# Two sparse expert layers: expert rows weighed at once and scattered with adding transfers onto stored residual rows

## What is computed

```python
x = x + gat(layernorm(x))
x = x + ffn0(layernorm(x))
x = x + gnn(layernorm(x))
x = x + ffn1(layernorm(x))

def ffn0(x):
    xn = norm(x) * gamma + beta
    top_vals, top_idx = top_k(xn @ Wr + br, 2)
    w = softmax(top_vals)                  # two shares for each node
    y = 0
    for e in range(8):
        h = gelu(xn @ W1[e] + b1[e])
        y = y + (h @ W2[e] + b2[e]) * w_full[..., e]
    return y
```

## Time and profile before

| | us |
|---|---|
| median of 3 runs | 3489.4 (3482.19 to 3492.77) |
| profiled execution, time | 3492.24 |
| profiled execution, span | 3490.5, mean granted TensorE clock 0.857 |

### The profile page before, as it was taken

One profiled execution on the slowest core, in us unless ns is written; L12 is line 12 of the kernel. 1 busy time (PEld: TensorE's weight loads), 2 busy tenths in 40 slices (PEclk: granted clock), 3 DMA queues, 4 the chain that ended last, 5 costly groups with the idle time before them and its releaser, 6 DMA issues. The chain is left out here.

```text
span 3490.5 us, 51176 instructions
## 1 busy us (share of the span) xinstructions
PE 2505.2 (72%) x12468; PEld 2001.2 (57%) x12469; DVE 1590.9 (46%) x3485; ACT 1320.4 (38%) x2875; POOL 1903.3 (55%) x2005
## 2 busy tenths in 40 slices
PE   5466666666666446999708888878888878649993
PEld 4344444444444435888607777767776744437772
DVE  5366666666666750111184444444444454621115
ACT  4544444444443223444343332332332324624441
POOL 0477777777775273222207777777777710553331
PEclk9688888887887557999959999999999999769996
DMA  5455555555553353222355555555555510432226
GB/s 154 126 140 140 143 140 140 144 140 141 144 140 94 100 194 100 82 82 84 112 184 167 159 158 153 158 159 153 158 159 152 151 32 2 140 130 85 91 85 251
DMA packets 319924, 459.47 MB, mean 132 GB/s; under 512 B 56729, under 2 KB 213962, under 8 KB 319498
## 3 DMA queue, kind: packets, MB, share of 16 engines
q0 software_dynamic: 94560, 261.75, 25.3%
q1 hardware_dynamic: 212888, 180.18, 17.6%
q10 hardware_dynamic: 12276, 15.62, 1.3%
HBM read 376.96 MB, written 80.39 MB: 131 GB/s over the span
## 5 line engine op out<-in xcount | busy, mean ns | idle before, releaser
L604 POOL DMA_INDIRECT room<-h_table,src_idx x784 | 749.1, 955 | 355.9 <-issue 238.3
L2182 POOL DMA_INDIRECT em_msg<-xn_table,src_idx x784 | 747.4, 953 | 337.5 <-issue 337.5
L1109 PE MATMUL at_ps<-room,at_member 128*128 128x264 f32 x1568 | 491.9, 468 | 68.7 <-DVE room L965 63.5
L2258 PE MATMUL em_pse<-em_We,em_attr_t 128*128 128x256 f32 x1552 | 396.1, 413 | 157.7 <-DVE em_msg L2206 157.7
L2206 DVE TENSOR_TENSOR em_msg<-em_pse,em_msg 128x1024 f32<-128x1024 f32 x196 | 230.8, 1219 | 551.3 <-DMA em_msg<-xn_table,src_idx 551.3
L2311 ACT ACTIVATE em_msg<-em_msg 128x1024 f32<-128x1024 f32 x196 | 207.2, 1057 | 682.7 <-DVE em_msg L2206 675.5
L2258 PEld LDWEIGHTS em_pse<-em_We,em_attr_t 128*128 128x128 f32 x1552 | 311.5, 206 | 226.4 <-DVE em_msg L2206 171.8
L1109 PEld LDWEIGHTS at_ps<-room,at_member 128*128 128x128 f32 x1568 | 339.6, 228 | 150.0 <-DVE room L965 82.1
L2265 PE MATMUL em_psa<-em_msg,em_member 128*128 128x256 f32 x1584 | 359.7, 380 | 4.4 <-DVE acc L2216 4.4
L2265 PEld LDWEIGHTS em_psa<-em_msg,em_member 128*128 128x128 f32 x1584 | 302.0, 191 | 46.2 <-DVE acc L2216 4.8
L1814 POOL DMA_INDIRECT y_table<-room,m0e_dest x104 | 99.7, 959 | 297.9 <-DVE room L1834 291.5
(11 more groups left out here) (402 smaller groups left out, 3863.0 us busy)
## 6 DMA issues: line engine op xcount, KB each, us to landing
em_attr<-in_edge_attr_dram SPq DMA_DIRECT2D x97, 512.0 KB, 4.2
room<-x_sorted SPq DMA_DIRECT2D x105, 258.0 KB, 2.7
at_dst_row<-dst_flat SPq DMA_DIRECT2D x98, 256.0 KB, 4.0
room<-h_table,src_idx POOLq DMA_INDIRECT x784
at_resets<-reset_flat SPq DMA_DIRECT2D x784, 8.0 KB
em_msg<-xn_table,src_idx POOLq DMA_INDIRECT x784, 2.8
room<-in_x_dram SPq DMA_DIRECT2D x12, 896.0 KB, 10.2
cn_rows<-y_table SPq DMA_DIRECT2D x5, 1792.0 KB, 10.2
```

The costliest lines, as they stand in the source:

```text
L604: pool.indirect_dma_start(msg[:, s, j, :], None, mem.h_table[:, :], bass.IndirectOffsetOnAxis(ap=mem.src_idx[:, c:c + 1].bitcast(u32), axi ...
L1109: ins = nc.tensor.matmul(sums[which], member[which][:, j, :], msg[:, s, c, :], start=(j == 0), stop=(j == CB - 1))
L2182: pool.indirect_dma_start(msg[:, s, j, :], None, mem.xn_table[:, :], bass.IndirectOffsetOnAxis(ap=mem.src_idx[:, c:c + 1].bitcast(u32), ax ...
L2258: ins = nc.tensor.matmul(ps_e[h][:, j, :], attr_t[:, s % 2, c * P:(c + 1) * P], We[:, :], start=True, stop=True)
```

## The change

The expert rows are multiplied by their share where they leave the experts, and the scatter adds them in HBM onto the residual row.

- Routing: as soon as a block's statistics are made, SP stores its residual rows to `m.target`, which is `y_table` for m0 (now one row for each node) and the output for m1. The shares are computed block by block: DVE makes `diff` in `choose`, ACT's new step `share(n)` the exponential as the last step of block n, and DVE the first share in `place`, into a third extra float of each scattered row. ACT's `share(n)` waits for `choose(n)`.
- Experts: DVE gets the destination by a copy, the share by two small operations (the second expert's share is one minus the first), and after the bias one multiplication for each tile. A new semaphore `y_taken` is set after the bias and is what PE waits for; `y_ready` is set after the multiplication. The scatter adds, and in m1 rows past the last node are dropped by a check of bounds.
- Home: m0 only loads the summed rows into `mem.X`, all loads issued at once, and goes on with the statistics. m1 has no such stage.

```diff
-XW = D + 2
+XW = D + 3
@@ phase_route, sync
+            for n in range(NR):
+                sp.wait_ge(var_ready, n + 1)
+                end = min((n + 1) * RT, m.target_rows // P)
+                sp.dma_start(m.target[n * RT * P:end * P, :].rearrange("(t p) f -> p t f", p=P),
+                             mem.X[:, n * RT:end, :]).then_inc(started, 16)
...
@@ phase_route, vector: choose and place
+                v.tensor_tensor(diff[:, tiles], top[1][:, tiles], top[0][:, tiles], ALU.subtract).then_inc(exp_in, 1)
...
+                dve.wait_ge(exp_done, n + 1)
+                chain(v.tensor_scalar(sums[:, tiles], ex[:, tiles], 1.0, None, ALU.add))
+                chain(v.reciprocal(xs[:, n % BUFS, :, D + 2], sums[:, tiles]))
                 dve.sem_inc(pos_ready, 1)
...
-            v.tensor_tensor(diff[:, :], top[1][:, :], top[0][:, :], ALU.subtract).then_inc(exp_in, 1)
-            dve.wait_ge(exp_done, 1)
-            chain(v.tensor_scalar(sums[:, :], ex[:, :], 1.0, None, ALU.add))
-            chain(v.reciprocal(m.w12[:, :, 0], sums[:, :]))
-            chain(v.tensor_tensor(m.w12[:, :, 1], m.w12[:, :, 0], ex[:, :], ALU.mult))
@@ phase_route, scalar
+            def share(n):
+                act.wait_ge(exp_in, n + 1)
+                tiles = slice(n * RT, (n + 1) * RT)
+                nc.scalar.activation(ex[:, tiles], diff[:, tiles], ACT.Exp).then_inc(exp_done, 1)
...
                     take_y(n + 3)
                 elif n == 0:
                     take_biases()
+                share(n)
@@ phase_experts, gpsimd
-                    pool.indirect_dma_start(mem.y_table[:, :], bass.IndirectOffsetOnAxis(ap=dest[:, j:j + 1].bitcast(u32), axis=0),
-                                            y[:, j, :], None).then_inc(sent, 16)
+                    pool.indirect_dma_start(m.target[:, :], bass.IndirectOffsetOnAxis(ap=dest[:, j:j + 1].bitcast(u32), axis=0),
+                                            y[:, j, :], None, bounds_check=m.last_row, oob_is_err=m.last_row is None,
+                                            compute_op=ALU.add).then_inc(sent, 16)
@@ phase_experts, vector
-                nc.vector.scalar_tensor_tensor(dest[:, :], of[:, :, 1], float(e), of[:, :, 0],
-                                               op0=ALU.not_equal, op1=ALU.add).then_inc(dest_ready, 1)
+                nc.vector.tensor_copy(dest[:, :], of[:, :, 0])
+                nc.vector.scalar_tensor_tensor(signed[:, :], of[:, :, 1], float(e), of[:, :, 2],
+                                               op0=ALU.not_equal, op1=ALU.subtract).then_inc(signed_ready, 1)
+                dve.wait_ge(signed_ready, g + 1)
+                nc.vector.scalar_tensor_tensor(share[:, :], signed[:, :], -1.0, signed[:, :],
+                                               op0=ALU.mult, op1=ALU.max).then_inc(dest_ready, 1)
                 for j in range(ET):
                     dve.wait_ge(y_done, g * ET + (j + 1))
-                    nc.vector.tensor_tensor(y[:, j, :], ps_y[:, j % 2, 0:D], m.b_last[:, e, :], ALU.add).then_inc(y_ready, 1)
+                    nc.vector.tensor_tensor(y[:, j, :], ps_y[:, j % 2, 0:D], m.b_last[:, e, :], ALU.add).then_inc(y_taken, 1)
+                    if j == 0:
+                        dve.wait_ge(dest_ready, g + 2)
+                    dve.wait_ge(y_taken, g * ET + (j + 3))
+                    nc.vector.tensor_scalar(y[:, j, :], y[:, j, :], share[:, j:j + 1], None, ALU.mult).then_inc(y_ready, 1)
@@ phase_experts, tensor
-                    pe.wait_ge(y_ready, g * ET + (j + 1))
+                    pe.wait_ge(y_taken, g * ET + (j + 1))
@@ phase_combine: removed
@@ phase_combine_norm: combine and weigh removed, loads straight into X
-            for n in range(1, BUFS):
+            for n in range(1, STEPS):
                 load(n)
             for n in range(STEPS):
-                if n + BUFS < STEPS:
-                    load(n + BUFS)
                 store(n)
```

More of the change, by code:

```diff
@@ L1346, in _ @@
                     load_x(n)
+            for n in range(NR):
[3 more added lines that the diff above has]
+                             mem.X[:, n * RT:end, :]).then_inc(started, 16)
+                if (n + 1) * RT * P > m.target_rows:
+                    sp.dma_start(m.target[end * P:m.target_rows, :], mem.X[0:m.target_rows - end * P, end, :]).then_inc(started, 16)
+            if m.attention is not None:
                 sp.wait_ge(heads_read, NR)
@@ L1822, in _ @@
             dve.sem_inc(y_ready, 2)
+            dve.sem_inc(y_taken, 2)
             dve.sem_inc(y_free, 1)
@@ L1897, in _ @@
             groups(act, group)
-def phase_combine(nc, mem, m, out=None):
-    TC, BUFS = 7, 3
-    SIZES = (3, 7, 7, 7, 7, 7, 5, 4, 2)
-    BLOCKS = [(sum(SIZES[:n]), nt) for n, nt in enumerate(SIZES)]
-    STEPS = len(BLOCKS)
-    with ExitStack() as ctx:
-        sb = lambda n, s, d=fp32: ctx.enter_context(nc.sbuf_tensor(f"{m.name}c_{n}", s, d))
-        sem = lambda n: new_semaphore(nc, mem, ctx, f"{m.name}c_{n}")
-        rows = sb("rows", [P, BUFS, TC, 2, D])
-        added, taken, stored = sem("added"), sem("taken"), sem("stored")
-        rows_in = [sem(f"rows_in{s}") for s in range(BUFS)]
-        block = ctx.enter_context(nc.Block(no_gpsimd_drain=True))
-        @block.vector
-        def _(dve):
-            for n, (t0, nt) in enumerate(BLOCKS):
-                s = n % BUFS
-                dve.wait_ge(rows_in[s], 16 * (n // BUFS + 1))
-                for w in range(2):
-                    for j in range(nt):
-                        t = t0 + j
-                        ins = nc.vector.scalar_tensor_tensor(tile_at(mem.X, t), rows[:, s, j, w, :], m.w12[:, t, w:w + 1],
-                                                             tile_at(mem.X, t), op0=ALU.mult, op1=ALU.add)
-                    if w == 0:
-                        ins.then_inc(added, 1)
-                        dve.wait_ge(added, n + 1)
-                ins.then_inc(taken, 1)
-            dve.wait_ge(taken, STEPS)
-        def load(eng, n):
-            t0, nt = BLOCKS[n]
-            s = n % BUFS
-            if n >= BUFS:
-                eng.wait_ge(taken, n - BUFS + 1)
-            at = t0 * P * 2
-            eng.dma_start(rows[:, s, 0:nt, :, :].rearrange("p t w f -> p t (w f)"),
-                          mem.y_table[at:at + nt * P * 2, :].rearrange("(t p w) f -> p t (w f)", p=P, w=2)).then_inc(rows_in[s], 16)
-        @block.scalar
-        def _(act):
-            for n in range(STEPS):
-                load(act, n)
-        @block.sync
-        def _(sp):
-            if out is not None:
-                for n, (t0, nt) in enumerate(BLOCKS):
-                    sp.wait_ge(taken, n + 1)
-                    end = min(t0 + nt, FULL_T)
-                    sp.dma_start(out[t0 * P:end * P, :].rearrange("(t p) f -> p t f", p=P),
-                                 mem.X[:, t0:end, :]).then_inc(stored, 16)
-                sp.dma_start(out[FULL_T * P:N, :], mem.X[0:TAIL, FULL_T, :]).then_inc(stored, 16)
-                sp.wait_ge(stored, 16 * (STEPS + 1))
@@ L2014, in then @@
                 dve.wait_ge(line, n_line[0])
-            def combine(n):
-                s = n % BUFS
-                dve.wait_ge(rows_in[s], 16 * (n // BUFS + 1))
-                for j in range(BLOCKS[n][1]):
-                    t = BLOCKS[n][0] + j
-                    ins = v.scalar_tensor_tensor(mem.X[:, t, :], rows[:, s, j, 0, :], m.w12[:, t, 0:1], mem.X[:, t, :],
-                                                 op0=ALU.mult, op1=ALU.add)
-                then(ins)
-                dve.wait_ge(weighed, n + 1)
-                v.tensor_tensor(mem.X[:, tiles_of(n), :], mem.X[:, tiles_of(n), :], rows[:, s, 0:BLOCKS[n][1], 1, :], ALU.add).then_inc(taken, 1)
-                dve.wait_ge(taken, n + 1)
             def row_stats(n):
+                dve.wait_ge(rows_in[n], 16)
                 for j in range(BLOCKS[n][1]):
@@ L2051, in _ @@
             for n in range(STEPS):
-                combine(n)
                 row_stats(n)
@@ L2063, in _ @@
         def _(act):
-            def weigh(n):
-                s = n % BUFS
-                act.wait_ge(rows_in[s], 16 * (n // BUFS + 1))
-                for j in range(BLOCKS[n][1]):
-                    t = BLOCKS[n][0] + j
-                    ins = nc.scalar.activation(rows[:, s, j, 1, :], rows[:, s, j, 1, :], ACT.Copy, scale=m.w12[:, t, 1:2])
-                ins.then_inc(weighed, 1)
             def normalize(n):
@@ L2092, in sparse_moe @@
         sb = lambda n, s, d=fp32: ctx.enter_context(nc.sbuf_tensor(f"{m.name}_{n}", s, d))
-        m.w12 = sb("w12", [P, NT, 2])
+        m.target = mem.y_table if out is None else out
+        m.target_rows, m.last_row = (NT * P, None) if out is None else (N, N - 1)
         m.plan = sb("plan", [1, 3, m.experts], i32)
```

34 lines of the change are left out of this document (13 added, 21 removed).

## The result

The changed kernel took 3575.5 us, median of 4 runs (3570.7 to 3578.9), against 3488.9 for the kernel before: ratio 1.0248, 95% interval 1.0236 to 1.026. It is 86 us slower where I had forecast 14 faster. Its profiled execution has a span of 3576.6 us against 3490.5.

| stage | before, us | after, us | difference | predicted |
|---|---|---|---|---|
| front and attention | 1155.3 | 1163.3 | +7.9 | 0 |
| m0 routing | 178.2 | 180.4 | +2.2 | +2 |
| m0 experts | 396.6 | 443.5 | +46.9 | 0 |
| m0 home | 96.1 | 60.0 | -36.0 | -33 |
| messages, hidden layer | 1119.4 | 1119.7 | +0.3 | 0 |

The account below looks back on a forecast made before the run. PE bounds m0's experts (7.34 us a group); m1's scatter loop runs almost as long as PE's 6.02. Homes -53.5 and -33, routing +11 and +2, m1's experts +58 sum to -15.5: 3475 us, range 3430 to 3575.

Parts of the forecast that it names:

- d: Expert scatter loops: extra time per group for adding in place of writing, taken at 0.9 us.
- -60 + 51 d: Whole kernel: change in us as a function of the price of adding; zero near 1.13, 52 more per us from 1.08.
- The bounds of d: Price of adding per group: at least zero; at most 4.7 us, a whole gather's 2.8 plus POOL's issue doubled twice.
- adding is dear: Rival, both expert stages: at d = 1.8 an 8.06 us loop bounds both, +70 us, 3559; chance 0.33.
- cover: m0's experts: PE's 7.34 us a group hides the scatter loop until d = 1.08; then 52 us per further us.
- The loop without the adding: Expert stages: scatter loop of 5.42 us plus 0.84 of new DVE work, 6.26 us a group.
- DVE's part: Expert loop, ahead of the first scatter: 0.33 small operations and wait, 0.41 multiplication, about 0.1 y_taken wait; 0.84 us.
- m0's experts at no cost: m0's experts: loop of 7.16 us stays hidden under PE's 7.34, so 0 us.
- The home stages: After the experts: m1's goes whole, -53.5 us; m0's loses DVE and ACT work, -33 us, to about 63.
- Routing: Routing stages: m1 +11 us as ACT's share(n) waits for choose(n), about 20 us a block; m0 +2.
- Early weights behind the stores: Routing, SP's queue: weights queue behind the target stores but land before POOL's last scatter; cost 0.
- gains don't come: Rival: m0's home stays transfer-bound, or TensorE gets less clock in m1's experts; each 10 to 20 us, 3492; chance 0.10.

Follow-up runs that it names:

- plain: The changed kernel with its scatters plain again, without adding, in both expert stages: 3435.3 us, ratio 0.9838.
- add_only_m1: The kernel before with only the scatters of m1's experts made adding, onto y_table; no weighing, home stages as before: 3574.8 us, ratio 1.0237.
- no_weighing: The changed kernel without the multiplication of y by its share and DVE's wait for dest_ready; the adding stays: 3555.3 us, ratio 1.0183.
- share_later: The changed kernel with ACT's exponential of block n's share moved into block n+1, behind the copy of the turned x: 3564.1 us, ratio 1.0221.
- early_add: The changed kernel plus one adding scatter of 128 rows onto y_table's pad rows at the end of POOL's front stage: 3564.1 us, ratio 1.0215.
- slots: The changed kernel with a landing semaphore for each y buffer; POOL waits for all scatters only where an expert begins: 3430.7 us, ratio 0.9825.
- the staged kernels: slots with the bias added into a tile of its own and all exponentials moved a block later: 3422.2 us; with an early adding scatter too: 3418.0 us.
- best: slots plus bias in a tile of its own, an early adding scatter, and exponentials moved for all blocks but the first: 3413.9 us, ratio 0.9776.

## Why the prediction was wrong

The form of the sum was right, and one term of it failed: d, the price of adding, taken at 0.9 us (0.6 for the landing and 0.15 for each of the two issues) and measured at 1.96. The prediction wrote the sum as -60 + 51 d, and 52 more for each us of d above 1.08. With 1.96 that is -60 + 100 + 46 = +86, and the medians differ by 86.6. That the two agree so closely is partly luck: without the rounding of its constant to -60 the sum gives 84, and +7.9 in attention is offset by smaller terms.

- **The bounds of d** were 0 and 4.7, and 1.96 lies between. Split as I split it, the two issues took 0.59 more each, 1.18 where I had 0.3, and the landing 0.78 beyond its issue where I had 0.6. So most of the miss, 0.88 of 1.06 us, is the issue, and the argument that failed is that it takes 0.96 us for scatters and gathers alike. That was no evidence on additions: both are 48 packets (the message gathers too, 7633 packets in 200 us for 159 of them), the addition is 144. No row of the kernel before showed the addition's. Whether the read of the destination runs beside the one from SBUF, as I assumed, no run here shows; the engines' time of 1.14 us instead of 0.36 shows only that the transfer did more than move its bytes twice.
- **The rival "adding is dear"**, d = 1.8 and 3559 us, is the mechanism that happened, and it was as good as level with my forecast (0.33 to 0.34). Its sum has a slip (104 + 37 is 141, not 143), which moves its time by 2 us. The sign turned at d = 1.13. At my d = 0.9 the loop had 0.18 us of cover left in m0 and none in m1, so d alone decided the sign. plain and add_only_m1 show it from both sides.
- **The loop without the adding** was right: 6.26 us predicted, 6.25 measured in plain. DVE's part was 0.84 predicted, and 0.73 in m0 and 0.84 in m1 measured. no_weighing puts the multiplication at 0.32 of it in m0's timeline, not 0.41.
- **m0's experts at no cost** failed with d: the cover of 1.08 us was read rightly, d went past it, and 46.9 us came out (52 x 0.88 = 46).
- **The home stages** were right: m1's -53.8 (predicted -53.5), m0's 60.0 us long (predicted 63).
- **Routing** was right in size: +8.6 and +2.2 (predicted +11 and +2). The cause in m1 is what I named: ScalarE waits for `choose(n)` (2.86 and 3.49 us in the lines above), a block takes 20.3 us (I had about 20), and share_later takes the waits of blocks 3 and 4 away. The blocks came out otherwise: I had 1.8, 5.1, 3.0 and 0.9 us more for blocks 1 to 4, and the traces show 0.8 less, then 2.5, 4.6 and 2.3 more. In m0 the +2.2 is right by luck. With the new routing but the fast issue, plain and early_add take 177.7 us, 0.5 less than the kernel before; with the old routing but the slow issue, add_only_m1 takes 179.8. So the new steps cost nothing there, and what shows is most likely the slower issue of its scatters.
- **Early weights behind the stores**: m1's experts started with the first load at 3145.25 and POOL's last routing scatter at 3141.2, so the stores cost nothing, as predicted.
- **The clock** fell in m1's experts, to 0.93, as in the rival "gains don't come", but PE was waiting there for the loop anyway, and with slots it is 1.00 again. PE's share of busy time alone doesn't explain it: in add_only_m1 PE was busy as long in the same stretch (127.66 us of 160 against 127.56) at a granted clock of 1.00, as its row shows. Why it fell stays open.

```profile
3220.00:3380.00 160.00, 127.66 (x608) 103.88 (x607) 18.49 (x63) 52.69 (x129) 67.65 (x44) 1.00 0.44 71
```

- **Attention's +7.9** I had not seen at all. 6.5 us of it are the gathers' issue (755.6 us busy against 749.1). plain, add_only_m1 and early_add rule out the tables' addresses.
- **The range** went up to d = 1.9 with 10 us more in routing, 3579, and I had rounded that down to 3575. The measured 3575.5 with d = 1.96 lies at this end, where the dear rival has the mechanism and my forecast doesn't.

## What to carry to other kernels

When a step is exchanged for one that the trace doesn't hold, look first at how much cover the loop has that it goes into. With less cover than the uncertainty of its price the sign of the change is open, and the remedy belongs to the change itself: here one landing semaphore for each buffer, in place of one for both, turned +2.5% into -1.75% at the same price of adding. And an engine that must wait for another engine's result should do so where its own queue holds nothing behind the wait that others need; share_later shows both sides of it, 11 us less behind the first block and 6 us more ahead of it. Last, a few us between two traces are a gain only if kernels that don't differ in that stretch agree better than that.

## What the runs showed of the hardware

- **An adding scatter of 128 rows of 1 KB** from SBUF to HBM: issue 1.55 us against 0.96, landing 3.8 us after issue against 2.4, 144 packets against 48, 1.14 us of each transfer engine against 0.36 (mean of the 16). It is the same into an internal table and into the output. With two in flight in their own loops it still lands in 3.8 us in slots, and in 3.8 to 4.0 in the staged kernels.
- **Plain indirect transfers issue more slowly until the first adding one has run.** In a kernel that holds adding scatters, the attention gathers, message gathers and routing scatters ahead of the first one take 953, 957 and 971 ns at the median; behind it, or in a kernel without adding ones, 946, 946 and 960. In the changed kernel attention is slow and the message gathers aren't; with the adding in m1 alone, both are slow; with one adding scatter in the front stage, neither is. It makes 7 to 11 ns each at the median, and 6.5 us over the 784 attention gathers. Three kernels (the changed one, add_only_m1, early_add) fix the rule, and the others follow it; why it is so, the traces don't show. In slots and in best the levels lie 3 ns higher throughout (957 and 949 ns for the attention gathers), which this rule doesn't explain.
